# First attention: scores over 64 partitions per head in alternating row groups, both transposed P copied by ACT

## The reference

```python
q = (x @ Wq).reshape(B, N, H, Dh).transpose(0, 2, 1, 3)
kv = x @ Wkv
k = kv[..., :H * Dh].reshape(B, N, H, Dh).transpose(0, 2, 1, 3)
v = kv[..., H * Dh:].reshape(B, N, H, Dh).transpose(0, 2, 1, 3)
s = jnp.einsum('bhid,bhjd->bhij', q * scale, k)
gm = jax.lax.stop_gradient(jnp.max(s, axis=-1, keepdims=True))
causal_mask = jnp.triu(jnp.ones((N, N), bool), 1)
p = jnp.where(causal_mask, 0.0, jnp.exp(s - gm))
num = jnp.einsum('bhij,bhjd->bhid', p, v)
out = num / (jnp.sum(p, axis=-1, keepdims=True) + EPS)
out = out.transpose(0, 2, 1, 3).reshape(B, N, H * Dh)
return out @ Wo + bo
```

## Time and profile before

| | us |
|---|---|
| median of 3 runs (2888.77 to 2889.01) | 2888.85 |
| the profiled execution | 2886.5 |
| its span | 2884.6 |
| TensorE busy over the span | 2635.6 (91%) |
| TensorE weight loads | 2275.2 (79%) |
| DVE busy | 1998.5 (69%) |
| ACT busy | 1464.2 (51%) |
| POOL busy | 589.8 (20%) |

### The profile page before, as it was taken

How to read it: one execution, slowest core, us unless ns; L and a number is a source line. 1 busy time by engine, 2 the same in 40 slices (tenths; PEclk the granted TensorE clock), 3 DMA queues, 4 the chain that set the end, 5 groups by cost and what they waited for, 6 DMA issues and landing times. The chain is left out here.

```text
span 2884.6 us, 66559 instructions
## 1 busy us (share of the span) xinstructions
PE 2635.6 (91%) x21306; PEld 2275.2 (79%) x21368; DVE 1998.5 (69%) x6252; ACT 1464.2 (51%) x4193; POOL 589.8 (20%) x1099
## 2 busy tenths in 40 slices
PE   5999999998999989999999899977998786899898
PEld 5988888897888789999999799965666465666576
DVE  4888888886777467777777677765776324677687
ACT  3666666665555456666666323323455222455543
POOL 0000000000111000000000011126776014777422
PEclk9999999998999999999999999988999797999999
DMA  5000000002000244444444100008553652655100
GB/s 143 2 2 1 1 1 1 1 1 62 2 0 0 89 134 147 146 147 146 147 148 148 32 1 0 0 21 232 158 151 95 90 70 78 165 154 152 46 14 17
DMA packets 196042, 212.13 MB, mean 74 GB/s; under 512 B 12628, under 2 KB 179940, under 8 KB 194420
## 3 DMA queue, kind: packets, MB, share of 16 engines
q1 hardware_dynamic: 195828, 209.64, 26.9%
HBM read 108.95 MB, written 90.65 MB: 69 GB/s over the span
## 5 line engine op out<-in xcount | busy, mean ns | idle before, releaser
L138 POOL TENSOR_TENSOR hT<-hT 128x256 fp32r<-128x256 f32 x64 | 46.9, 733 | 1466.3 <-ACT hT L131 1466.3
L122 PE MATMUL bank<-hT,a_xA 128*128 128x256 f32 x768 | 227.3, 296 | 5.0 <-ACT a_p L459 2.8
L123 PE MATMUL bank<-hT,a_xA 128*128 128x256 f32 x768 | 216.6, 282 | 0.0
L124 PE MATMUL bank<-hT,a_xA 128*128 128x256 f32 x768 | 216.0, 281 | 0.0
L602 DVE TENSOR_REDUCE a_nmax<-bank 128x2 f32<-128x512 f32 x256 | 174.9, 690 | 56.0 <-PE bank L124 53.7
L1706 ACT ACTIVATE a_p<-bank 128x1024 f32<-128x1024 f32 (+1 forms) x256 | 193.5, 808 | 23.9 <-PE bank L1761 17.7
L1069 ACT ACTIVATE a_p<-a_p,a_nmax 128x256 f32<-128x256 f32 x256 | 128.1, 501 | 133.5 <-DVE a_nmax L1253 133.5
L480 ACT CAST a_xA<-bank 128x256 fp32r<-128x256 f32 x256 | 95.0, 373 | 197.3 <-PE bank L124 197.3
L1334 ACT ACTIVATE f_silu<-bank 128x512 f32<-128x512 f32 x128 | 76.5, 598 | 213.8 <-PE bank L124 213.8
L799 ACT ACTIVATE f_hidden<-bank,arena 128x256 f32<-128x256 f32 x256 | 120.5, 473 | 114.6 <-PE bank L124 113.4
L862 PE MATMUL bank<-arena,f_hidden 128*128 128x128 f32 x1024 | 172.0, 288 | 6.4 <-DVE f_acc L916 5.0
(11 more groups left out here) (304 smaller groups left out, 8346.6 us busy)
## 6 DMA issues: line engine op xcount, KB each, us to landing
pos_dram<-a_pos SPq DMA_DIRECT2D x128, 383.0 KB, 2.4
a_stack<-rows_dram SPq DMA_DIRECT2D x128, 320.0 KB, 4.1
rows_dram<-a_cut SPq DMA_DIRECT2D x192, 192.0 KB, 2.4
a_shifted<-pos_dram SPq DMA_DIRECT2D x128, 256.0 KB, 2.6
f_merged<-f_staged SPq DMA_DIRECT2D x16, 578.0 KB, 9.0
gate<-gates_dram SPq DMA_DIRECT2D x32, 256.0 KB, 11.1
arena<-in_task SPq DMA_DIRECT2D x4, 1156.0 KB, 8.5
x<-in_x SPq DMA_DIRECT2D x4, 512.0 KB, 8.6
```

The costliest lines, as they stand in the source:

```text
L122: pe.matmul(out, left[0], right[0], start=start, stop=False, skip_group_check=True)
L123: pe.matmul(out, left[0], right[1], start=False, stop=False, skip_group_check=True)
L124: return pe.matmul(out, left[1], right[0], start=False, stop=stop, skip_group_check=True)
```

## The change

The product A is given up. q and k of each head are computed as such, for two heads at once, and the scores of a head are taken over its 64 features: head 0 lies on partitions 0 to 63, head 1 on 64 to 127, and the twelve score matmuls alternate between the two. V is made from the rounded parts by `matmul3` for two steps' heads at once, one half of the tokens in each step. The weights are cut in six pieces at the start of the phase in place of the sixteen products. ACT now copies the transposed P of both heads. `s_mm` is raised once for each step, and the scores wait for both rests and both heads' exponentials.

```diff
-        A = ctx.enter_context(nc.sbuf_tensor("a0_A", [P, 2 * PER, 2, P], F32R))
-        xA = ctx.enter_context(nc.sbuf_tensor("a0_xA", [P, 4, 2, T], F32R))
-        v = sb("v", [P, 4, NT, P])
+        W = ctx.enter_context(nc.sbuf_tensor("a0_W", [P, 3, 2, 1024], F32R))
+        qk = ctx.enter_context(nc.sbuf_tensor("a0_qk", [P, 2, 2, 2, T], F32R))
+        v = sb("v", [P, 4, NT, 2 * P])
...
+        def piece(i):
+            x, first = i % 3, i // 3 * 512
+            return w[("wq0", "wk0", "wv0")[x]][:, first:first + 512], x, slice(first, first + 512), 1.0 if x else 64 ** -0.5
...
             def _(act):
-                for h in range(2 * PER):
-                    act.wait_ge(s["A_mm"], h + 1)
-                    act.activation(A[:, h, 0, :], k.banks[h % 4][:, 0:P], ACT.Identity, scale=64 ** -0.5
-                                   ).then_inc(s["A_rounded"], 1)
+                act.wait_ge(k.weights_in[phase], 16 * weight_pieces(phase))
+                for i in range(6):
+                    whole, x, part, scale = piece(i)
+                    act.activation(W[:, x, 0, part], whole, ACT.Identity, scale=scale).then_inc(s["W_rounded"], 1)
...
                     if b2.real:
+                        wait(act, s["pT_mm"], b2, 2, 1)
+                        wait(act, s["o_mm"], b2.shift(-2))
+                        act.copy(pT[:, b2.ring(2), 0, :], pT_ps[0][:, 0:C]).then_inc(s["pT0"], 1)
                         wait(act, s["pT_mm"], b2, 2)
-                        wait(act, s["o_mm"], b2.shift(-2))
                         act.copy(pT[:, b2.ring(2), 1, :], pT_ps[1][:, 0:C]).then_inc(s["pT1"], 1)
...
                     if nx.real:
-                        wait(act, s["s_mm"], nx.shift(-2), 2)
-                        for h in range(2):
-                            wait(act, s["xA_mm"], nx, 2, 1 - h)
-                            act.copy(xA[:, 2 * nx.ring(2) + h, 0, :], xA_ps[h][:, 0:T]).then_inc(s["xA_rounded"], 1)
-                        wait(act, s["o_mm"], nx.shift(-4))
-                        act.copy(v[:, nx.ring(4)], xA_ps[1][:, T:2 * T].rearrange("p (t d) -> p t d", t=NT)).then_inc(s["v"], 1)
+                        wait(act, s["s_mm"], nx.shift(-2))
+                        for i in range(2):
+                            wait(act, s["qk_mm"], nx, 2, 1 - i)
+                            act.copy(qk[:, nx.ring(2), i, 0, :], qk_ps[i][:, 0:T]).then_inc(s["qk_rounded"], 1)
+                        wait(act, s["o_mm"], nx.shift(-7 - nx.p % 2))
+                        act.copy(v[:, nx.s // 2 % 4, nx.p % 2, :], qk_ps[1][:, T:2 * T]).then_inc(s["v"], 1)
...
             def _(pe):
-                for h in range(2 * PER):
-                    if h >= 4:
-                        pe.wait_ge(s["A_cut"], h - 3)
-                    pe.matmul(k.banks[h % 4][:, 0:P], w["wqT0"][:, h, :], w["wkT0"][:, h, :], start=True, stop=True
-                              ).then_inc(s["A_mm"], 1)
-                pe.wait_ge(s["A_cut"], 2 * PER)
+                pe.wait_ge(s["W_cut"], 6)
...
                     if at.real:
-                        for h in range(2):
-                            wait(pe, s["xA"], at, 2, 1 - h)
-                            wait(pe, s["exp"], at.shift(-1), 2, 1 - h)
-                            for t in range(NT):
-                                mm = matmul3(pe, s_ps[h][:, t * T:(t + 1) * T],
-                                             halves(xA, 2 * at.ring(2) + h, t * P, (t + 1) * P),
-                                             halves(n.hT2, at.s // PER % 2, 0, T), start=(t == 0))
-                            mm.then_inc(s["s_mm"], 1)
+                        wait(pe, s["qk"], at, 2)
+                        wait(pe, s["exp"], at.shift(-1), 2)
+                        for t in range(NT):
+                            for a, c in ((0, 0), (0, 1), (1, 0)):
+                                for h in range(2):
+                                    mm = pe.matmul(s_ps[h][:, t * T:(t + 1) * T],
+                                                   qk[64 * h:64 * h + 64, at.ring(2), 0, a, t * P:(t + 1) * P],
+                                                   qk[64 * h:64 * h + 64, at.ring(2), 1, c, :],
+                                                   start=(t == 0 and a == 0 and c == 0), stop=(a == 1),
+                                                   skip_group_check=True)
+                        mm.then_inc(s["s_mm"], 1)
...
                     if nx.real:
-                        for h in range(2):
-                            wait(pe, s["xA"], nx.shift(-1), 2, 1 - h)
-                            for t in range(NT if h else 0):
-                                pe.matmul(xA_ps[1][:, T + t * P:T + (t + 1) * P], n.hT[:, item, t * P:(t + 1) * P],
-                                          w["wv0"][:, c:c + P], start=True, stop=True)
-                            matmul3(pe, xA_ps[h][:, 0:T], halves(A, 2 * nx.p + h, 0, P), halves(n.hT2, item, 0, T)
-                                    ).then_inc(s["xA_mm"], 1)
+                        t, first = nx.p % 2, nx.p // 2 * 2 * P
+                        for i in range(2):
+                            wait(pe, s["qk"], nx.shift(-1), 2, 1 - i)
+                            if i:
+                                matmul3(pe, qk_ps[1][:, T:2 * T], halves(n.hT2, item, t * P, (t + 1) * P),
+                                        [W[:, 2, part, first:first + 2 * P] for part in range(2)])
+                            matmul3(pe, qk_ps[i][:, 0:T], [W[:, i, part, nx.p * P:(nx.p + 1) * P] for part in range(2)],
+                                    halves(n.hT2, item, 0, T)).then_inc(s["qk_mm"], 1)
...
             def _(dve):
-                for h in range(2 * PER):
-                    dve.wait_ge(s["A_rounded"], h + 1)
-                    dve.scalar_tensor_tensor(out=A[:, h, 1, :], in0=k.banks[h % 4][:, 0:P], scalar=64 ** -0.5,
-                                             in1=A[:, h, 0, :], op0=ALU.mult, op1=ALU.subtract).then_inc(s["A_cut"], 1)
+                for i in range(6):
+                    whole, x, part, scale = piece(i)
+                    dve.wait_ge(s["W_rounded"], i + 1)
+                    dve.scalar_tensor_tensor(out=W[:, x, 1, part], in0=whole, scalar=scale, in1=W[:, x, 0, part],
+                                             op0=ALU.mult, op1=ALU.subtract).then_inc(s["W_cut"], 1)
...
-                    if b2.real:
-                        wait(dve, s["pT_mm"], b2, 2, 1)
-                        wait(dve, s["o_mm"], b2.shift(-2))
-                        dve.tensor_copy(pT[:, b2.ring(2), 0, :], pT_ps[0][:, 0:C]).then_inc(s["pT0"], 1)
                     if at.real:
                         for h in range(2):
-                            wait(dve, s["s_mm"], at, 2, 1 - h)
+                            wait(dve, s["s_mm"], at)
...
                     if nx.real:
-                        for h in range(2):
-                            if h == 0:
-                                wait(dve, s["xA_rounded"], nx, 2, 1)
+                        for i in range(2):
+                            if i == 0:
+                                wait(dve, s["qk_rounded"], nx, 2, 1)
                             else:
                                 wait(dve, s["v"], nx)
-                            dve.tensor_tensor(xA[:, 2 * nx.ring(2) + h, 1, :], xA_ps[h][:, 0:T],
-                                              xA[:, 2 * nx.ring(2) + h, 0, :], ALU.subtract).then_inc(s["xA"], 1)
+                            dve.tensor_tensor(qk[:, nx.ring(2), i, 1, :], qk_ps[i][:, 0:T],
+                                              qk[:, nx.ring(2), i, 0, :], ALU.subtract).then_inc(s["qk"], 1)
```

More of the change, by code:

```diff
@@ L365 @@
 WEIGHTS = [
-    [("wqT0", (16, P), 64), ("wkT0", (16, P), 64), ("wv0", (1024,), P), ("wo0", (8, P), P), ("bo0", (P,), P)],
+    [("wq0", (1024,), P), ("wk0", (1024,), P), ("wv0", (1024,), P), ("wo0", (8, P), P), ("bo0", (P,), P)],
     [("e1w", (16, P), P), ("e2w", (16, P), P), ("e1b", (16,), P), ("rw", (15,), P), ("rb", (15,), P),
@@ L414, in attention0 @@
         rec = sb("rec", [P, 2, 2, NT])
-        xA_ps = k.banks[0:2]
+        qk_ps = k.banks[0:2]
         s_ps, pT_ps = k.banks[2:4], k.banks[4:6]
         o_ps, y_ps = k.banks[6], k.banks[7]
-        names = ("chain", "var", "std", "rstd", "xn", "ht_mm", "ht", "ht_rounded", "ht_cut", "A_mm", "A_rounded", "A_cut",
-                 "xA_mm", "xA_rounded", "xA", "v", "s_mm",
+        names = ("chain", "var", "std", "rstd", "xn", "ht_mm", "ht", "ht_rounded", "ht_cut", "W_rounded", "W_cut",
+                 "qk_mm", "qk_rounded", "qk", "v", "s_mm",
                  "nmax", "masked", "exp", "den", "rec", "p", "pT_mm", "pT0", "pT1", "o_mm", "oT", "y_mm", "res")
@@ L473, in step @@
                             wait(act, s["ht_mm"], ni, item=True)
-                            modulated(act, k, phase, ni, xA_ps[0][:, T:2 * T], n.hT[:, ni.s // PER % 2, :], s["ht"])
```

(33 more changed lines are left out.)

## The result

The changed kernel took 2870.3 us, the median of 4 runs (2868.7 to 2870.4), against 2888.8 for the kernel before beside it: a ratio of 0.9935 (0.9918 to 0.9952), some 18.5 us less. The forecast had the sign and a range that holds it; the gain was forecast at 28 us. In the profiled executions the span went from 2884.6 to 2868.7 us.

The account below looks back on a forecast made before the run. TensorE was taken to bound the first attention stage. 8 x 4.60 + 1.6 = 38.4 us per item, 4.80 per step in place of 5.02; 127 x 0.22 = 28 us off the median gave 2861 us, range 2838 to 2892.

Parts of the forecast that it names:

- Scores: First attention stage, TensorE: twelve score matmuls in pairs, 0.12 us a pair, 0.71 us less; 0.89 us with 0.09 added behind.
- rival of serial halves: Score matmuls: the two array halves run one after the other, 5.45 us per step, +55, 2944 us; chance 0.12.
- load rule: Skill's rule for TensorE weight loads: time follows columns, not rows, 107 ns for 128; twelve on one path need 1.28 us.
- slow rivals: Score matmuls: halves one after the other (2944 us, 0.12) or loads half hidden (2906 us, 0.08); slower, together 0.20.
- The entry into another shape: TensorE's price for reshaping its array around the scores: 0.09 us added behind them, bounds 0 and 0.3 us.
- TensorE's own work: TensorE's instructions in one step of the stage, without waits: 4.20 us, where the step before was 4.92.
- Loop through the maxima: Scores, DVE's maxima, second mask at 2.45 (TensorE waits 0.38), P.V, projection, transposes, next scores: 4.60 us, the longest loop.
- Loop through the exponentials: Scores wait for both heads' exponentials on ACT: masks at 1.95, exponentials 0.72 later, lasting 1.74; 4.46 us with handover.
- Item ends: Extra time per item, from DVE's late work, modulation at p = 5 and loop's turn: 1.6 us in place of 0.8.
- Start of the stage: Six weight cuts replace sixteen small matmuls, DVE then waits for the gate: nothing either way, at most 2 us gained.
- half-hidden loads: Score matmuls' weight loads only half hidden, a pair at 0.19 us: 5.15 us per step, +17, 2906 us; chance 0.08.
- dear item ends: Item ends cost twice as much, 3.2 us per item: 5.00 us per step, about no change, 2886 us; chance 0.06.

## Why the prediction was right, and its size off

**Scores.** 0.90 us against 0.89: a pair takes one slot. The rival of serial halves is out by the row of L522. What is out is that the two halves' loads share one path. The load rule itself holds in that a load over 64 partitions takes as long, 187 ns, as one over all 128 in the kernel before, 188 to 190; the formula's 107 ns doesn't. The Trainium skill's page "TensorE: Matmul & The Clock Gate", in the section "Packing small matmuls — row/col tiling", says that loads overlap matmuls in flight only when the row group differs. The twelve loads started within 0.6 us agree with the overlap, and the experiment without the alternation, 1.25 us, shows that the order counts. The "only" doesn't hold here. In the kernel before a full-height load starts at 319.47, while the first score matmul (319.38 to 319.75) is in flight over the same rows:

```profile
319.47 0.19 PEld L123 LDWEIGHTS bank<-hT,a_xA 128*128 128x128 f32 x1
```

Read beside the load rule, that section would still have taken most of the 0.20 from the slow rivals.

**The entry into another shape** is the term that was mis-sized. I had put it at "the slow first slot after the transposes" plus 0.09 behind the scores. From the transposes to the scores there are 0.75 us (325.68 to 326.43) against 0.58 in the earlier trace rows: the scores start 0.07 before the transposes' modelled end. This is not the wait for the exponentials, which end 0.15 before these scores. At p = 5 they end 0.52 before (at 349.90), and the distance from the transposes is 0.74 to 0.75 all the same:

```profile
349.67 0.23 ACT L463 ACTIVATION_READ_ACCUMULATOR a_p<-bank,a_nmax 128x1 f32 x1
349.68 0.82 PE L383 MATMUL bank<-ident,a_p 128*128 128x128 f32 x6
350.42 0.39 PE L522 MATMUL bank<-a_qk 64*128 64x256 f32 x2
```

P.V, another shape too, starts at 324.33 with the last mask's end at 324.40, the same 0.07. Behind the scores the 0.09 was there, in the block's 0.90, but the first full product then takes 0.23 as well (322.65 to 322.88) in place of 0.12. Together 0.17 + 0.09 + 0.11 = 0.37 us, above my upper bound of 0.3: the whole gap ahead of the eight P.V instructions was no bound for the way into and out of scores. TensorE's own work is 4.68 less its wait for the second mask, 324.11 - 323.88 - 0.06 = 0.17: 4.51, not 4.20. The Trainium skill says in "TensorEngine Tiling (Array Packing)", section "Key Properties", that a change of mode drains the engine. The trace agrees in that both ways cost time, 0.17 us on the way in and 0.20 on the way out.

**Loop through the maxima.** The maxima start at 1.01 (0.99 forecast) and last 1.29, not 1.41: that row of before had a wait for head 1's scores within it. The second mask is at 2.36, not 2.45. Then come 0.22 to P.V, 0.80, 0.55 and 0.75: 4.68, not 4.60. Two errors, -0.09 and +0.17, and the wait before the mask is 0.17, not 0.38: 21.3 us in the stage, not 45.

**Loop through the exponentials.** It was forecast at 4.46, below the other, and is just as long. Masks at 2.07, not 1.95 (the 0.11 above, from the first full product); the exponentials at 2.80; their end at 326.28, 4.53; the scores 0.15 later, where I had put 0.05 from the mask behind DVE's maxima. Sum 4.68. P.V between the masks showed it. The loop through DVE ends at 4.30 (326.05) and binds nothing; it was forecast at 4.40.

**The P copy** is hidden in the plain step, as forecast. **V** is worth 0.1 us, as forecast, through the loop of the exponentials.

**Item ends.** Forecast 1.6 us per item, 25.6 in all; measured 8 x (4.89 - 4.68) = 1.7, or 26.9. That the two agree is luck, for the parts do not. The three late steps of an item cost 0.21, 0.37 and 0.25, 0.83 in all against 1.05, or 12.5 us where I had 16.8. The turn costs 1.67 to 1.93 us, 1.79 in the mean, and there are five, 8.9 us; I had eight of 1.1. I had it on DVE, and it is ACT's: the second idle time, 1.80 us, is right ahead of the two P copies, and P.V waits 1.36 for them. The first two steps, which I had at nothing, cost 4.7 us over plain ones (7.73 + 6.32 - 2 x 4.68), and 1.3 in the kernel before. They ran at the lower clock; 1.28 us are a table load of ACT (L461), which both kernels have. I had written that a lower clock in the stage would make every term wrong; it did so for these two steps. The 0.8 us that are left lie in small excesses of single steps.

**Start of the stage.** Forecast at nothing, it cost 2.06 us: 0.88 because the gate's transfer came later (DVE's first xn at 43.14 against 42.26), the rest because the first scores now wait for the rests of q and k of both heads (TensorE idle 1.20 us before them, ended by DVE's L627). The two slow steps behind it are counted above.

**The sum.** Against the profiled execution 28 us were forecast and 15.9 of the span came. The 12 between them are 127 x 0.08 = 10.2 for the plain step (the entry, and the handover from ACT), 16 x 0.1 = 1.6 for what comes on top of plain steps, 2.1 for the start, and 2.0 the other way behind the stage. Against the medians 9 us are missing, since the profiled execution of before lay 2.35 us under its median and that of after on its own. Of the 15.9 us, 2.0 lie in code that the change does not touch and are luck. The mechanism stood; the entry was mis-sized, and the wait at the second mask, 0.38 us in the forecast, took up 0.21 of the 0.31 us that TensorE's own work came out longer. The rivals of half-hidden loads (a pair at 0.19) and of dear item ends (3.2 us per item) are out by their rows.

## What to carry to other kernels

Two half-height matmuls in row halves cost one slot if they are issued in turn, and lose over half of the gain if not (0.35 of 0.61 us here); each way into and out of another shape cost some 0.2 us, so count these and not only slots. Where a new bound lies only a few hundredths of a microsecond above the next, work out each loop with its handovers, and expect that one edit for one loop gives nothing: test them together. And before a few microseconds are put down to a change in a looped stage, look whether the idle time at the loop's turn came or went with the position of the code, whether the clock rose at the same time in both, and what the code behind the stage took.

## What the runs showed of the hardware that I had not expected

The idle time at the turn of a loop came and went with twenty small copies ahead of it: 5.1 and 8.8 us over five turns on ACT, or none. ACT has 228 recorded instructions per lap of two items, 341 with the waits and register instructions. The Trainium skill's page "Runtime: NRT & Kernel Launch", section "Instruction fetch mechanics", says that code is fetched in blocks of 256 instructions, two of which are held, and that a taken branch to a target outside of them stalls the engine. The rows fit that and don't prove it: no row names a fetch, and why unchanged code behind the stage takes 2182 to 2197 us from kernel to kernel stays open too.

The order of the halves is not all or nothing. Issued one head after the other, twelve matmuls took 1.25 us, not 1.51.

A single register instruction of TensorE's sequencer ahead of a wait cost 0.09 us per step, right behind a mask that had waited: 0.24 from the mask to P.V in the hardware loop, where the instruction is there, and 0.15 outside of it, where it is not.

A matmul that waits for ACT's last read of the sums starts 0.14 us after that read's end (328.24 to 328.38, with P.V between the masks); one behind DVE's maxima 0.06 (324.05 to 324.11).
